# A vision block on one core: the output projection as ten products, `att` made in two multiplies, and three pieces of order moved

## What is computed

```python
h = tok_ref(x, tok_W, tok_b)                  # (128, 196, 192)
h = concatenate([cls_tok, h], axis=1)         # (128, 197, 192)
h = h + attention(layernorm(h), Wq, Wk, Wv, Wo, anchor_w, anchors, lam)
h = h + ffn(layernorm(h), weight_t, bias)
# attention: softmax(q k^T * 32**-0.5 + lam * (q . anchor)) v, then @ Wo.T
# ffn: clip(round(x / 0.02), -128, 127) @ weight_t * 0.0002 + bias
```

## Time and profile before

| | |
|---|---|
| median of three runs | 1881.69 us (1878.8 to 1881.96) |
| profiled execution | 1878.63 us, span 1876.9 us |
| TensorE busy | 1752.2 us (93%) |
| VectorE busy | 1413.3 us (75%) |
| ScalarE busy | 781.9 us (42%) |
| GpSimd busy | 740.3 us (39%) |

### The profile page before, as it was taken

The page is one execution under the profiler, slowest core; times in us unless marked ns, Lnnn a source line. Parts: engine busy times, 40 slices in busy tenths (PEclk is TensorE's granted clock), DMA queues, the critical chain, the costliest instruction groups (busy, mean ns, idle before and its releaser), DMA issues.

```text
span 1876.9 us, 51604 instructions
## 1 busy us (share of the span) xinstructions
PE 1752.2 (93%) x15344; PEld 1597.9 (85%) x15344; DVE 1413.3 (75%) x3646; ACT 781.9 (42%) x1878; POOL 740.3 (39%) x1910
## 2 busy tenths in 40 slices
PE   1999999992799999999999999999999999999995
PEld 1999999992688888888888888888888888888884
DVE  4888888883477777777777777777777777777773
ACT  2000000000355555555555555555555555555552
POOL 3343453452044343443434434344343443434434
PEclk8999999996899999999999999999999999999997
DMA  9789999954777777787777777778777787777751
GB/s 281 215 277 303 310 316 280 310 211 108 112 129 137 140 134 134 129 134 139 134 135 128 134 139 134 135 128 134 139 134 135 128 133 138 135 136 127 135 99 30
DMA packets 214779, 303.57 MB, mean 162 GB/s; under 512 B 47584, under 2 KB 203635, under 8 KB 204612
## 3 DMA queue, kind: packets, MB, share of 16 engines
q1 hardware_dynamic: 204542, 227.27, 64.0%
q10 hardware_dynamic: 6054, 38.54, 7.2%
q0 software_dynamic: 4128, 37.06, 5.1%
HBM read 126.49 MB, written 58.29 MB: 98 GB/s over the span
## 4 chain that ended last, share of the span: by engine, by line
issue 30%; POOL 23%; PE 9%; DVE 8%; POOLq 3%; DMA 1%; SPq 1%; ACT 0%; DVEq 0%; ACTq 0%
POOL hb L1198 6%; POOL ln L146 4%; POOL qx L1216 4%; DVE h L1129 3%; DVE qx L1118 2%; PE o_bank L863 2%; PE bank L803 2%; POOLq L1208 2%; POOL ln L139 1%; POOL ln L145 1%; POOL ln L143 1%; POOL ln L147 1%; POOL ln L144 1%; POOL ln L141 1%; POOL ln L142 1%
## 5 line engine op out<-in xcount | busy, mean ns | idle before, releaser
L1078 DVE TENSOR_REDUCE neg_max<-bank 99x2 f32<-99x394 f32 x768 | 419.9, 560 | 243.7 <-PE bank L835 242.5
L1005 ACT ACTIVATE probs<-bank 99x396 f32<-99x396 f32 x768 | 383.5, 499 | 278.6 <-PE bank L847 278.4
L317 PE MATMUL bank<-e_t,xt 128*128 128x192 f32 x2352 | 388.3, 329 | 39.0 <-DVE xt L403 22.4
L317 PEld LDWEIGHTS bank<-e_t,xt 128*128 128x128 f32 x2352 | 386.8, 192 | 40.3 <-DVE xt L403 23.5
L847 PE MATMUL bank<-q_st,k_st 98*99 98x198 f32 x1536 | 284.5, 267 | 11.2 <-DMA q_st<-max_rows 6.1
L863 PE MATMUL o_bank<-probs,vals 99*64 99x198 f32 (+1 forms) x3072 | 290.3, 337 | 0.4 <-issue 0.3
L835 PE MATMUL bank<-k_st,q_st 96*99 96x198 f32 x1536 | 275.1, 274 | 7.5 <-issue 3.3
L863 PEld LDWEIGHTS o_bank<-probs,vals 99*64 99x64 f32 (+1 forms) x3072 | 213.0, 137 | 48.6 <-issue 1.1
L847 PEld LDWEIGHTS bank<-q_st,k_st 98*99 98x99 f32 x1536 | 202.5, 166 | 59.0 <-issue 36.5
L403 DVE STREAM_TRANSPOSE xt<-x_t 128x256 f32<-128x256 f32 x588 | 214.9, 416 | 44.7 <-PE bank L317 44.2
L999 ACT ACTIVATE x_hi<-bank 128x396 fp32r<-128x396 f32 x128 | 63.3, 495 | 414.2 <-PE bank L784 414.2
(11 more groups left out here) (121 smaller groups left out, 3340.3 us busy)
## 6 DMA issues: line engine op xcount, KB each, us to landing
x_t<-in_x_dram ACTq DMA_DIRECT2D x26, 1344.0 KB, 18.3
x_t<-in_x_dram SPq DMA_DIRECT2D x26, 1344.0 KB, 22.1
q_st<-qk_hi SPq DMA_DIRECT2D x128, 198.0 KB, 4.2
k_st<-qk_hi SPq DMA_DIRECT2D x128, 198.0 KB, 4.7
xn_in<-xn_scratch SPq DMA_DIRECT2D x128, 148.5 KB
h_in<-h_scratch SPq DMA_DIRECT2D x128, 148.5 KB
h_scratch<-h_t POOLq DMA_DIRECT2D x13, 1344.0 KB, 17.6
xn_scratch<-xn_t POOLq DMA_DIRECT2D x13, 1344.0 KB, 8.2
```

The lines of the kernel that those rows point to most:

```text
L317: last = pe.matmul(token_bank(p)[:, 0:D], xt[:, p, c // 3, c % 3, :], e_t[:, row_kind(t), col, c // 3, c % 3, :], start=c == 0, stop=c == 5)
L1005: nc.scalar.activation(probs[:, n.two, h, :, :], wide(T_BANK, TC), ACT.Exp).then_inc(exp_done, 1)
L1078: nc.vector.tensor_reduce(out=neg_max[:, n.two, :, h], in_=wide(S_BANK[h % 2], TC)[:, :, 0:NTOK], axis=AX_X, op=ALU.max, negate=True).then ...
```

## The change

The weights of the output projection are laid out, loaded and split like those of q, k and v (a fourth entry in `wa_hi`, `wa_lo`, `wb`, `wb_rest`), and `project_output` takes five products for each half of the tokens: three over 128 rows, one over 128 stacked rows, one over 97. For the stacking `att` gets 256 columns: VectorE writes all heads into the first 192 and the last two heads once more behind them, as a second multiply, and the turn of `att` waits for both. `a_hi` and `a_lo` have 128 partitions; `a_lo` is made in two pieces, and its rows 64 to 96 are cleared once.

In VectorE's step maximum 3 goes behind the quantization, and the statistics of `h1` go ahead of `x_lo` and `a_lo`. In SyncE's step the load of `xn` comes first, seven images ahead and into one of three buffers. The store of the last row's first eight tokens of `xn` moves from GpSimd's queue to SyncE's, and GpSimd waits for VectorE's last rows of `xn` before it clears `k_st`.

```diff
-                pool.dma_start(xn_dram[:, bass.ds(at_token, T), :] if last else xn_dram[:, bass.ds(at_token, G), :],
-                               xn_t[:, 0:T if last else G, :]).then_inc(xn_stored, 16)
+                if not last:
+                    pool.dma_start(xn_dram[:, bass.ds(at_token, G), :], xn_t[:, 0:G, :]).then_inc(xn_stored, 16)
...
             sp.wait_ge(biases_landed, 32)
+            at_token = (G - 1) * G + 1
+            sp.wait_ge(ln_step, G * LN_PER)
+            sp.dma_start(xn_dram[:, at_token:at_token + EARLY, :], xn_t[:, 0:EARLY, :]).then_inc(early_stored, 16)
...
             def load_xn(n):
-                if n.reuses(NS):
-                    sp.wait_ge(xt_done, n.count(1, 1 - NS))
+                if n.reuses(NX):
+                    sp.wait_ge(xt_done, n.count(1, 1 - NX))
...
-                f, p, a, c, k, ahead = i.plus(5), pair_of(i), i.plus(1), i.plus(-1), i.plus(-4), i.plus(6)
+                f, p, a, c, k, ahead = i.plus(5), pair_of(i), i.plus(1), i.plus(-1), i.plus(-4), i.plus(7)
                 if i.fixed and i.n == -5:
                     load_xn(f)
+                    load_xn(f.plus(1))
+                if ahead.within(B):
+                    load_xn(ahead)
...
-                if ahead.within(B):
-                    load_xn(ahead)
...
             def project_output(bank, n):
                 for c in range(2):
-                    acc = bank[0:TC, c * D:(c + 1) * D]
-                    for ic in range(2):
-                        hi = a_hi[:, n.two, ic, c * TC:(c + 1) * TC]
-                        lo = a_lo[:, n.two, ic, c * TC:(c + 1) * TC]
-                        pe.matmul(acc, hi, wo_hi[:, ic, :], start=ic == 0, stop=False)
-                        pe.matmul(acc, hi, wo_lo[:, ic, :], start=False, stop=False)
-                        last = pe.matmul(acc, lo, wo_hi[:, ic, :], start=False, stop=ic == 1)
+                    tokens = slice(c * TC, (c + 1) * TC)
+                    xa_hi, xa_lo = a_hi[:, n.two, 0, tokens], a_lo[:, n.two, 0, tokens]
+                    pairs = ((wa_hi[:, O, :], xa_hi), (wa_lo[:, O, :], xa_hi), (wa_hi[:, O, :], xa_lo),
+                             (wb[:, O, :], a_hi[:, n.two, 1, tokens]), (wb_rest[:, O, :], a_lo[0:BIAS_LO + 1, n.two, 1, tokens]))
+                    for i, (weights, inputs) in enumerate(pairs):
+                        last = pe.matmul(bank[0:TC, c * D:(c + 1) * D], inputs, weights, start=i == 0,
+                                         stop=i == len(pairs) - 1)
...
-                    pe.wait_ge(norm_done, c.count(1, 1))
-                    turn(o_bank[:, 0, :], att, c, DC).then_inc(at_done, 1)
+                    pe.wait_ge(norm_done, c.count(2, 2))
+                    turn(o_bank[:, 0, :], att, c.two, DA).then_inc(at_done, 1)
...
-                if has_a:
-                    maxima(a, 3)
                 if has_g:
                     dve.wait_ge(ln2_step, g.count(LN2_PER, LN2_PER))
...
+                if has_a:
+                    maxima(a, 3)
                 if has_e:
...
-                    nc.vector.tensor_tensor(att[:, c.two, :, :].rearrange("p c (h d) -> p c h d", h=H),
-                                            heads[:, :, :, 0:HD], inv.unsqueeze(3).broadcast_to([TC, 2, H, HD]),
-                                            ALU.mult).then_inc(norm_done, 1)
+                    for heads_in, at in (((0, H), 0), ((H - 2, H), D)):
+                        part = slice(heads_in[0], heads_in[1])
+                        many = heads_in[1] - heads_in[0]
+                        nc.vector.tensor_tensor(
+                            att[:, c.two, :, at:at + many * HD].rearrange("p c (h d) -> p c h d", h=many),
+                            heads[:, :, part, 0:HD], inv[:, :, part].unsqueeze(3).broadcast_to([TC, 2, many, HD]),
+                            ALU.mult).then_inc(norm_done, 1)
...
+                if has_e:
+                    dve.wait_ge(h1_done, e.count(1, 1))
+                    for cc in range(2):
+                        last = nc.vector.bn_stats(st2[:, e.two, cc, :], h1[:, e.two, cc, :])
+                    last.then_inc(st2_done, 1)
                 if has_f:
                     dve.wait_ge(xhi_done, f.count(1, 1))
...
-                    nc.vector.tensor_tensor(a_lo[:, c.two, :, :], wide(o_bank[:, 0, :], DC),
-                                            a_hi[:, c.two, :, :].bitcast(F32), ALU.subtract).then_inc(alo_done, 1)
-                if has_e:
-                    dve.wait_ge(h1_done, e.count(1, 1))
-                    for cc in range(2):
-                        last = nc.vector.bn_stats(st2[:, e.two, cc, :], h1[:, e.two, cc, :])
-                    last.then_inc(st2_done, 1)
+                    for ic, rows_in in enumerate((DA, DB)):
+                        last = nc.vector.tensor_tensor(a_lo[0:rows_in, c.two, ic, :], wide(o_bank[:, 0, :], rows_in)[:, ic, :],
+                                                       a_hi[0:rows_in, c.two, ic, :].bitcast(F32), ALU.subtract)
+                    last.then_inc(alo_done, 1)
...
+            nc.vector.memset(a_lo[DB:BIAS_LO + 1, :, 1, :].bitcast(F32), 0.0).then_inc(a_zeroed, 1)
...
+            pool.wait_ge(last_row_xn, G - EARLY)
             pool.memset(k_st[ST:ST + 2, :, :, :, :].bitcast(F32), 1.0).then_inc(ones_made, 1)
```

More of the change, by code:

```diff
@@ L163, in build_tokens @@
     tok_bias = sb("tok_bias", [B, D], F32, tokens)
-    w_raw = sb("w_raw", [DA, 3, 2, D], F32, tokens)
-    wo_raw = sb("wo_raw", [DC, 2, D], F32, tokens)
+    w_raw = sb("w_raw", [DA, 4, 2, D], F32, tokens)
     ffn_raw = sb("ffn_raw", [DC, 2, D], I8, tokens)
@@ L357, in _ @@
             high(ffn_raw[:], ffn_w_bf[:], w_high)
-            for i in (Q, K, V):
+            for i in (Q, K, V, O):
                 scale = {"scale": SCALE} if i == K else {}
@@ L637, in build_attention @@
     inv_sum = tile("inv_sum", [TC, NS, 2, H])
-    att = tile("att", [TC, NS, 2, D])
-    a_hi = tile("a_hi", [DC, NS, 2, TP], F32R)
-    a_lo = tile("a_lo", [DC, NS, 2, TP], F32R)
+    att = tile("att", [TC, NS, 2, DA + 2 * DB])
+    a_hi = tile("a_hi", [DA, NS, 2, TP], F32R)
+    a_lo = tile("a_lo", [DA, NS, 2, TP], F32R)
     h_in = tile("h_in", [TC, NS, 2, D])
@@ L779, in _, with turn @@
         def _(pe):
-            def turn(bank, src, n, width):
+            def turn(bank, src, at, width):
                 for ic in range(2):
@@ L784, in turn @@
                         last = pe.transpose(bank[0:width, ic * TP + c * TC:ic * TP + (c + 1) * TC],
-                                            src[:, n.two, c, ic * width:(ic + 1) * width], ident[0:TC, 0:TC])
+                                            src[:, at, c, ic * width:(ic + 1) * width], ident[0:TC, 0:TC])
                 return last
@@ L856, in attend @@
                 if n.reuses(1):
-                    pe.wait_ge(norm_done, n.count(1, 0))
+                    pe.wait_ge(norm_done, n.count(2, 0))
                 for p in range(HP):
@@ L953, in step @@
                         pe.wait_ge(xlo_done, f.count(1, 0))
-                    turn(MISC[2], xn_in, f, DA).then_inc(xt_done, 1)
+                    turn(MISC[2], xn_in, f.slot % NX, DA).then_inc(xt_done, 1)
                 if has_a:
@@ L964, in step @@
                         pe.wait_ge(qxt_done, k.count(1, 1))
-                    turn(MISC[0], qx, g, DC).then_inc(qt_done, 1)
+                    turn(MISC[0], qx, g.two, DC).then_inc(qt_done, 1)
                 if has_c:
-                    pe.wait_ge(norm_done, c.count(1, 1))
-                    turn(o_bank[:, 0, :], att, c, DC).then_inc(at_done, 1)
+                    pe.wait_ge(norm_done, c.count(2, 2))
+                    turn(o_bank[:, 0, :], att, c.two, DA).then_inc(at_done, 1)
                 if has_a:
@@ L1047, in step @@
                         act.wait_ge(op_done, c.count(1, 1 - NS))
-                    copy(a_hi[:, c.two, :, :], wide(o_bank[:, 0, :], DC), ahi_done)
+                    copy(a_hi[:, c.two, :, :], wide(o_bank[:, 0, :], DA), ahi_done)
                 if has_b:
```

52 lines of the change are left out of this document (24 added, 28 removed).

## The result

The changed kernel takes 1871.51 us (median of six runs, 1870.06 to 1874.06) against 1879.13 us for the kernel before in the same comparison: a ratio of 0.9958, 95% interval 0.9945 to 0.997. It is 0.4% faster; forecast was 1883.0, no gain. The profiled execution took 1870.06 us with a span of 1868.04 us, 8.86 us less than the span before.

The account below looks back on a forecast made before the run. TensorE's loop was taken to bound odd steps, GpSimd's chain even ones. 1878.63 + 11.8 (pairs) - 9.3 (between stages) - 1.4 (loads) + 0.2 (first stage) = 1879.9, plus 3.06 for the median: 1883.0 us, range 1866 to 1896.

Parts of the forecast that it names:

- Two loops bound the steps: Attention steps: TensorE's loop bounds the odd step (10.73 us), GpSimd's chain from statistics to `qx` the even one (10.56 us).
- Ten products -0.18 in the odd step only: Output projection: two fewer products save 0.18 us in the odd step; in the even step they only lengthen a wait.
- Second multiply +0.20 in every step: VectorE's doubling of attention's last heads: taken as 0.28 us long, it delays TensorE's turn of `att` by 0.20 us every step.
- Statistics ahead of `x_lo`: VectorE's step: GpSimd starts 1.03 us earlier, while `x_lo` and block 0 start 0.53 us later, lengthening the odd step.
- +0.20 us a pair: Attention's odd and even step together: +0.55 and -0.35 us, over some 59 pairs +11.8 us.
- Maximum 3 behind the quantization +0.48 in the even step: VectorE's even step: maximum 3 now stands between quantization and `h1`, costing 0.48 us; nothing in the odd step.
- Between the stages: Gap from tokens to attention: moving the `xn` store and delaying the `k_st` clearing together save 9.3 us.
- Rival (3): Gap between stages closes only in part, as SyncE's store or small clearings wait: +1.6 to +5.6 us, chance 0.16.
- Token loads: Head of SyncE's step: no steady cost, -1.4 us at attention's start, where rows of maxima are awaited.
- Rival (2): Token loads delay k's stacks, so a pair's first score waits 0.6 us: +35 us, 1918 us, chance 0.08.
- The end: Stretch from the last turn of `att` to the kernel's end: the sum put no change there, 0 us.

Follow-up runs that it names:

- stats_back: The changed kernel with the statistics of `h1` behind `a_lo` again in every step; 1953.49 us, ratio 1.0383.
- mixed_order: The changed kernel with maximum 3 ahead of the quantization, statistics ahead of `x_lo` only at odd blocks' end, otherwise between `x_lo` and `a_lo`; 1842.42 us.
- twelve_products: The changed kernel with one product of 128 rows repeated in each half of the output projection, twelve products again; 1891.06 us, ratio 1.0056.
- loads_back: The changed kernel with token loads in their old place of SyncE's step, two buffers, six images ahead; 1877.58 us, ratio 0.9987.
- max3_back: The changed kernel with maximum 3 ahead of the quantization again; 1871.23 us, ratio 0.9945.
- by_parity: The changed kernel with statistics ahead of `x_lo` only at odd blocks' end, otherwise behind `a_lo`, maximum 3 still behind the quantization; 1881.5 us, ratio 0.9999.
- mixed_hoisted: mixed_order with `x_lo`'s second wait, for v's products, moved ahead of the maxima's parts; 1848.04 us, ratio 0.9836.
- wait_ahead: The changed kernel with `x_lo`'s second wait, for v's products, moved ahead of the statistics; 1874.36 us, ratio 0.9963.
- store_sync: The kernel before with only the last early store of `xn` moved to SyncE's queue; 1876.23 us, ratio 0.9983.
- loads_first: The kernel before with only the token loads moved to the head of SyncE's step, three buffers, seven images ahead; 1877.09 us, ratio 0.9989.
- clear_last: The kernel before with only GpSimd waiting for VectorE's six rows of `xn` before clearing `k_st`; 1878.38 us, ratio 0.999.

## Why the prediction was wrong

- *Two loops bound the steps.* Right: stats_back shows GpSimd's alone, mixed_order shows TensorE's restored in the odd step.
- *Ten products -0.18 in the odd step only.* Right for the step from before to after; beside the shorter GpSimd chain the even step counts 0.16 as well (twelve_products), which no sum against the kernel before could use.
- *Second multiply +0.20 in every step.* Right, 0.28 us long.
- *Statistics ahead of `x_lo`.* This is the step that failed. The mechanism is right; the term was mis-sized, and with it "+0.20 us a pair", which measured +0.05. I had moved `x_lo` by one pair of statistics (0.53) and kept the 0.17 us that stood ahead of it; they shrank to 0.09. Block 0 starts 2.98 us behind A for 2.52 (forecast 3.05), and TensorE idles 0.40 us ahead of it where I had said some 0.7. GpSimd starts 2.39 us behind A for 3.46, 1.07 sooner (forecast 1.03), and its `qx` ends 1.10 sooner, 0.02 of this by the token loads (loads_back). So each step in the loop is some 0.08 us shorter than the sum has it, and in unrolled code, where before had no such gap, the sum is exact. The earlier trace rows are rows of the loop; what lay between the parts and `x_lo` was not among them.
- *Maximum 3 behind the quantization +0.48 in the even step.* The even step came out as the sum says, `h1` 8.61 us behind A for 9.22. But max3_back shows that the order of the two is then worth nothing: the earlier chain took away the idle time in which maximum 3 ran, and the term is the price of that, not of its place.
- *Between the stages.* Right in kind: -8.3 us for -9.3, the block ending 1.3 us behind VectorE and not 0.3. One behind the other, the six rows take 1.82 us for 7.61. VectorE's small clearings at 433.64 and 434.86 run at 0.59 and 0.39 us each while GpSimd's of 6.03 us is under way; by the Trainium skill (SBUF — State Buffer, Who interferes with whom) they take no shared port, and the trace agrees. Rival (3) held for 1 us of its 1.6 to 5.6.
- *Token loads.* Rival (2) fell: no score of the loop waits for a stack. The 10.8 us in the page after are one wait, ahead of the first score of all at 463.70 (before: 2.57 us at 473.58). It is longer only because TensorE is through with the next image's tokens sooner; that score starts 24.0 us behind the first turn, before 24.1. The gain was undersized: 3.0 us at the start for 1.4, and 0.03 us in each even step for nothing.
- *The end.* Put at nothing in the sum without a reason, -1.76 us. VectorE of the kernel before, last block but one, and of after:

```profile
1855.25 0.56 DVE L1140 TENSOR_TENSOR att<-o_bank,inv_sum 99x384 f32<-99x384 f32 x1
1856.98 0.57 DVE L1168 TENSOR_TENSOR a_lo<-o_bank,a_hi 96x396 fp32r<-96x396 f32 x1 [1.17 <-ACT a_hi L999]
1857.46 0.61 DVE L1173 BATCH_NORM_STATS2 st<-h 99x6 f32<-99x192 f32 x2
```

```profile
1847.95 0.75 DVE L1144 TENSOR_TENSOR att<-o_bank,inv_sum 99x384 f32<-99x384 f32 x2
1848.62 0.61 DVE L1163 BATCH_NORM_STATS2 st<-h 99x6 f32<-99x192 f32 x2
1849.88 0.62 DVE L1179 TENSOR_TENSOR a_lo<-o_bank,a_hi 128x198 fp32r<-128x198 f32 x2 [0.66 <-ACT a_hi L1000]
```

When no maxima and no `x_lo` are left, the old order makes the statistics stand behind `a_lo` and its wait for `a_hi`; they start 2.2 us behind the start of `att`, in the new order 0.7, and GpSimd's chain, through which the last images go to the end, follows them. All kernels with the statistics first in that place end 19.2 to 19.3 us behind their last A; stats_back and by_parity, like before, 21.0 to 21.4.

Summed: the 54 pairs in the loop took 2.7 us more than before, where the sum had 10.8, a miss of 8.1 us. The 19 unrolled steps took 1.7 us more for the 1.0 that the sum had for five more pairs, 0.8 us the other way. That makes the 7.3 between first and last A. The end adds 1.8, and the start 1.1, which is luck: without the 1.5 us by which the first stage happened to end earlier the start would have missed the other way. What makes after faster than before, 8.86 us of span, are the start and the end (13.3 us, these 1.5 of luck included); between first and last A the change costs 4.5 us.

## What to carry to other kernels

Two steps of a software pipeline that alternate need not be bound by the same loop; find the loop of each, and give each the order that serves it: here one `if` by parity was worth 36 us, more than the whole change. A move that helps one loop and holds the other shows as almost no change, and is easily taken for work off the path. When an instruction is moved, its own length is not the whole shift: count from start to start, with the waits that stand ahead of it, and compare a step of the loop with an unrolled one.

## What the runs showed of the hardware that I had not expected

- In the loop `x_lo`, behind a VectorE instruction of 0.17 us and with two waits ahead of it, started 0.08 us later than in unrolled code (0.17 for 0.09 us in before, 0.16 or 0.17 in mixed_order). With one of the waits taken away it started at 0.09 to 0.10 (mixed_hoisted); the statistics with two waits ahead of them at 0.09 (wait_ahead). One wait more ahead of the parts cost 0.06 us, in the loop and out of it (mixed_hoisted).
- GpSimd's last store held its block's end for 4.63 us before GpSimd went on the earlier trace rows; the same store on SyncE's queue leaves 2.99 us of idle time, of which 1.4 are behind VectorE's last instruction (store_sync). The end of a block has its cost either way.
- The granted clock at the kernel's end differs from one profiled execution to the next and is worth as much as the edits of the start: the last two steps take 18.29 us at a clock of 1.00 (mixed_order) and 25.63 us at 0.59 (loads_first). That the two groups of clear_last, 6 us apart, come from there too fits their mean clocks but is not shown, since only one of its executions was profiled. The table of windows (TensorE's busy time with its count, clock, DMA share, GB/s) of the kernel before and of loads_first:

```profile
1840.00:1857.00 17.00, 14.43 (x110) 0.83 0.14 37
```

```profile
1840.00:1857.00 17.00, 15.71 (x88) 0.50 0.07 19
```

In loads_first the clock is at its lower level, 1.2 GHz (0.50), through the whole stretch; its last two steps are 12.78 and 12.85 us long, in the kernel before 11.28 and 10.07, so 4.3 us of its profiled 1880.95 us come from there and hide its gain of 3 at the start. TensorE had been busy 22.31 of the 25 us ahead (1815 to 1840) in it and 22.12 in the kernel before, so I can't say from these rows what decides it. For an edit worth a few microseconds the stretches of one trace told more than medians did.
